# Graph layer and expert layer on one core: row numbers of the first chunk found on chip, down products ahead of the third tile's up products, turned halves kept apart

## The reference, cut

```python
def ln(x): ...                                   # over the 1024 columns
h   = ln(x) @ W.T + b                            # x 1250 x 1024
agg = segment_sum(norm[:, None] * h[col], row)   # 20000 edges and one loop per node
x   = x + agg
y   = ln(x)
logits = y @ router_w.T + router_b               # 8 experts
topk_vals, topk_idx = top_k(logits, 2); topk_w = softmax(topk_vals)
for e in range(8):                               # w1 512 x 1024, w2 1024 x 512
    cw  = sum(where(topk_idx == e, topk_w, 0), -1)
    out = out + (gelu(y @ w1[e].T + b1[e]) @ w2[e].T + b2[e]) * cw[:, None]
return x + ln_w_b(out + y)
```

## Time and profile before

| | us |
| --- | --- |
| median of the runs | 623.88 (621.68 to 625.24) |
| span of the profiled execution | 619.0 |
| PE busy in the span | 533.6 (86%) |
| DVE busy | 470.0 (76%) |
| ACT busy | 242.4 (39%) |
| POOL busy | 193.9 (31%) |
| aggregate loop | 183 to 283.9 |
| first chunk up to the second chunk's up products | 283.9 to 343.7 |

### The profile page before, as it was taken

The page is one execution under the profiler, slowest core; times in us unless marked ns, Lnnn a source line. Parts: engine busy times, 40 slices in busy tenths (PEclk is TensorE's granted clock), DMA queues, the critical chain, the costliest instruction groups (busy, mean ns, idle before and its releaser), DMA issues.

```text
span 619.0 us, 12317 instructions
## 1 busy us (share of the span) xinstructions
PE 533.6 (86%) x3660; PEld 298.1 (48%) x3661; DVE 470.0 (76%) x1295; ACT 242.4 (39%) x358; POOL 193.9 (31%) x199
## 2 busy tenths in 40 slices
PE   1688999899999999995779999999999999999100
PEld 1244554445444555554564655556565656564000
DVE  8879869997174889898858778695868685755397
ACT  5333444324280243435534344343444443401470
POOL 3013000000001165656544535344452543151240
PEclk9999999999899999998699999999999999999655
DMA  6894320333327243445486969798897889173978
GB/s 234 326 380 139 58 46 10 72 77 60 57 95 279 103 158 141 167 138 201 127 303 168 271 211 233 251 231 254 219 263 200 260 222 284 28 166 77 263 209 279
DMA packets 59565, 112.34 MB, mean 181 GB/s; under 512 B 33490, under 2 KB 33903, under 8 KB 59504
## 3 DMA queue, kind: packets, MB, share of 16 engines
q1 hardware_dynamic: 49424, 80.02, 37.7%
q0 software_dynamic: 8896, 27.38, 21.3%
q10 hardware_dynamic: 1184, 4.20, 2.0%
HBM read 71.75 MB, written 33.67 MB: 170 GB/s over the span
## 4 chain that ended last, share of the span: by engine, by line
PE 77%; DVE 14%; issue 3%; DMA 2%; ACT 2%; DVEq 1%; POOL 0%; ACTq 0%; POOLq 0%; SPq 0%
PE ps L1794 7%; PE ps L1795 7%; PE ps L1913 7%; PE ps L1914 6%; PE ps L1915 6%; PE ps L1892 5%; PE ps L1893 5%; PE ps L1894 5%; PE ps L1703 4%; PE ps L1642 4%; PE ps L1705 4%; PE ps L1704 4%; PE ps L1874 4%; DVE wbufs L1279 2%; PE ps L1623 2%
## 5 line engine op out<-in xcount | busy, mean ns | idle before, releaser
L613 POOL DMA_INDIRECT acc_rows<-work,ids_out x24 | 53.0, 2208 | 106.1 <-DVE work L1497 106.1
L1794 PE MATMUL ps<-wbufs,rows_and_counts 128*128 128x512 f16 x200 | 75.8, 379 | 0.5 <-DVE wbufs L1279 0.5
L1892 PE MATMUL ps<-rows_and_counts,wbufs 128*128 128x336 f16 (+2 forms) x256 | 74.9, 298 | 1.4 <-DVE rows_and_counts L1437 0.8
L1795 PE MATMUL ps<-wbufs,rows_and_counts 128*128 128x512 f16 x200 | 75.8, 379 | 0.0
L1893 PE MATMUL ps<-rows_and_counts,wbufs 128*128 128x336 f16 (+2 forms) x256 | 74.9, 298 | 1.0 <-issue 1.0
L1894 PE MATMUL ps<-rows_and_counts,wbufs 128*128 128x336 f16 (+2 forms) x256 | 74.9, 298 | 0.0
L1913 PE MATMUL ps<-wbufs,rows_and_counts 128*128 (+1 forms) x192 | 72.9, 379 | 1.6 <-issue 1.3
L1452 DVE SCALAR_TENSOR_TENSOR wbufs<-stage,wbufs 128x1024 f16<-128x1024 f32 x56 | 67.2, 1218 | 8.4 <-ACT wbufs L927 8.3
L1914 PE MATMUL ps<-wbufs,rows_and_counts 128*128 (+1 forms) x192 | 72.8, 379 | 0.0
L1915 PE MATMUL ps<-wbufs,rows_and_counts 128*128 (+1 forms) x192 | 72.8, 379 | 0.0
L526 POOL TENSOR_TENSOR work<-work 128x1024 f16<-128x1024 f32 x9 | 19.2, 2130 | 168.9 <-ACT work L900 168.9
(11 more groups left out here) (308 smaller groups left out, 1054.1 us busy)
## 6 DMA issues: line engine op xcount, KB each, us to landing
stage<-wst_in SPq DMA_DIRECT2D x72, 512.0 KB
acc_rows<-work SPq DMA_DIRECT2D x10, 512.0 KB
x_rows<-work SPq DMA_DIRECT2D x10, 512.0 KB
t<-x_in SPq DMA_DIRECT2D x1, 4096.0 KB, 14.0
wbufs<-b_in ACTq DMA_DIRECT2D x8, 512.0 KB
wbufs<-acc_rows SPq DMA_DIRECT2D x8, 512.0 KB, 6.2
t<-x_in SPq DMA_DIRECT2D x1, 3072.0 KB, 11.6
t<-x_in SPq DMA_DIRECT2D x1, 2048.0 KB, 7.8
```

Source lines behind the costliest of these rows:

```text
L1794: mm(o, ct_hi[:, cs], hs[:, at:at + HALF], start=(m == 0), stop=False, skip_group_check=True)
L1795: mm(o, ct_hi[:, cs], hs[:, D + at:D + at + HALF], start=False, stop=False, skip_group_check=True)
L1892: mm(o, wbufs[:, ds(w + ws, P)], x_hi, start=(j == 0), stop=False)
```

## The change

- Row numbers of the first chunk are found on chip. For each tile DVE sums the two masks of expert 0 (`chosen`) and compares the tile's slots with 0 to 383 (`slot_hot`, 128x384 in f16, only the third tile's columns from tile 7 on); PE multiplies that with a column of row numbers (`number`, three products one column wide); DVE adds the tiles up (`ids_known`). SP's two reads of the slot table for it go. POOL gathers the first two tiles in iteration 8 (before: 9, behind the aggregate's end), the third in iteration 11.
- DVE places tile 6 inside `add_agg(8)`, tile 7 between the halves of `add_agg(9)`, and chooses for tile 8 behind the normalized row of tile 9. PE ranks tile 7 inside `aggregate(9, 1)`.
- The weight pieces of expert 0 are split in iterations 0 to 7 (before: 2 to 9), on POOL directly behind `xs_lo` and ahead of the scatters.
- Turned halves stay apart: high and low are transposed into places of their own in PSUM, in f16. For a row tile ACT copies the high half and DVE the low one; for a chunk ACT copies both and DVE's subtractions (L1365, L1437) go.
- First chunk: PE multiplies the first two tiles up between the last turnings, goes down for tile 0 (parts 0 and 1), turns the third tile, part 2, third tile up, part 3, then turns the second chunk between parts 4 and 5. The gelus of the first two tiles come on their own. On DVE two pieces stand ahead of the halves of the first two tiles.

```diff
@@ POOL, the loop
             for r in range(NT + 2):
                 if r < NT - 1:
                     xs_lo(NT + r)
+                if r < PIECES:
+                    split_lo(PIECES + r, e_hi[0], e_lo[0])
                 if 2 <= r:
-                    if r - 2 == FIRST_TILES:
-                        pool.wait_ge(agg_done, 2 * NT)
+                    if r - 1 == FIRST_TILES:
                         pool.wait_ge(x2_first_stored, 16 * FIRST_TILES)
-                        pool.wait_ge(ids_in, 16)
+                        pool.wait_ge(first_ids_done, 1)
                         for i in FIRST:
-                            gather_first(i, ids_first, FIRST_TILES)
+                            gather_first(i, ids_known, FIRST_TILES)
+                    if r == NT + 1:
+                        ...
+                        pool.wait_ge(third_id_done, 1)
+                        ...
                     pool.wait_ge(slots_done, r - 1)
                     ...
-                if 2 <= r < NT:
-                    split_lo(PIECES + r - 2, e_hi[0], e_lo[0])
@@ ACT, the loop (the high half of the piece moves in the same way)
-            for r in range(NT + 1):
+            for r in range(NT):
                 ...
+                if r < PIECES:
+                    split_hi(PIECES + r, e_hi[0])
+            turn_copied(0)
+            turn_copied(1)
+            x2t_hi(NT - 1)
+            turn_copied(2)
+            turn_copied(3)
             act.wait_ge(gap_done, 1)
@@ DVE
             def x2t_lo(r):
-                dve.wait_ge(x2t_hi_done, r + 1)
-                v.tensor_tensor(x2t[:, D:], x2t_ps, x2t[:, 0:D], ALU.subtract).then_inc(x2t_lo_done, 1)
+                dve.wait_ge(x2t_done, r + 1)
+                dve.wait_ge(router_done, r)
+                v.tensor_copy(x2t[:, D:], x2t_ps[1]).then_inc(x2t_lo_done, 1)
@@
+                    if r == NT - 1 and n == 0:
+                        place(r - 2)
                 ...
+                if r == FIRST_TILES + 1:
+                    place(FIRST_TILES - 1)
                 ...
                 if r == NT - 1:
-                    x2t_lo(r - 1)
+                    choose(r - 1)
@@
-            def place(r):
+            def number_slots(r):
                 dve.wait_ge(rank_done, r + 1)
+                st3.did(v.tensor_tensor(chosen[:], choice(r)[:, 0:1], choice(r)[:, NE:NE + 1], ALU.add))
                 st3.link(v.tensor_tensor(slot_of[:], rank_ps[:, 0:NE], carry[:], ALU.add))
+                if r >= 2:
+                    dve.wait_ge(slot_hot_used, r - 1)
+                first = 0 if r < FIRST_TILES else FIRST_CH
+                v.tensor_scalar(slot_hot[r % 2][:, first:], slot_no16[:, first:], slot_of[:, 0:1], chosen[:],
+                                ALU.is_equal, ALU.mult).then_inc(slot_hot_done, 1)
+
+            def place_slots(r):
                 st3.link(v.tensor_tensor(slot_pick[:]...
@@
             for r in range(NT + 2):
-                if 2 <= r:
+                if r == FIRST_TILES + 2:
+                    dve.wait_ge(slot_hot_used, FIRST_TILES)
+                    st3.link(v.tensor_reduce(ids_sum[:, 0:len(FIRST)], ids_ps[:, 0:len(FIRST), 0:FIRST_TILES], AXX, ALU.add))
+                    v.tensor_copy(ids_known[:, 0:len(FIRST)], ids_sum[:, 0:len(FIRST)]).then_inc(first_ids_done, 1)
+                if 2 <= r and r != NT:
                     choose(r - 2)
@@
+            def first_chunk(split):
+                st4.enter(0)
+                for j in range(2):
+                    piece_lo(0, j, split)
+                for f in range(FK):
+                    dve.wait_ge(first_gelu_done, f + 1)
+                    halves_of(slice(f * CH, f * CH + FIRST_CH)).then_inc(y_lo_first, 1)
+                ...
+                for k in range(3):
+                    evict(0, k, 0)
+                    if 2 + k < EARLY:
+                        piece_lo(0, 2 + k, split)
+                for f in range(FK):
+                    dve.wait_ge(gelu_done, FK + f + 1)
+                    halves_of(slice(f * CH + FIRST_CH, (f + 1) * CH)).then_inc(y_lo_done, 1)
+                evict(0, 3, 0)
+                ...
@@ PE
+            def number(r):
+                pe.wait_ge(slot_hot_done, r + 1)
+                for i in range(CT) if r < FIRST_TILES else range(len(FIRST), CT):
+                    ins = mm(ids_ps[:, i, r:r + 1], slot_hot[r % 2][:, i * P:(i + 1) * P], token16[:, r:r + 1],
+                             start=True, stop=True)
+                ins.then_inc(slot_hot_used, 1)
@@
-            for r in range(NT + 2):
-                ...
+            for r in range(NT):
+                aggregate(r, 0)
+                if r >= 4:
+                    number(r - 4)
+                if r == FIRST_TILES + 2:
+                    number(FIRST_TILES - 1)
+                    pe.wait_ge(first_ids_done, 1)
                 if r >= 2:
                     route(r - 2)
+                if r == NT - 1:
+                    aggregate(r, 1, range(NT - 3))
+                    rank(r - 2)
+                    aggregate(r, 1, range(NT - 3, NT))
+                    turn2(r - 1)
+                    continue
+                aggregate(r, 1)
+                if r >= 1:
+                    turn2(r - 1)
                 if r >= 2:
                     rank(r - 2)
+            number(NT - 3)
+            route(NT - 2)
+            turn_first(0)
+            turn_first(1)
+            rank(NT - 2)
+            turn2(NT - 1)
+            up_first(0)
+            number(NT - 2)
+            route(NT - 1)
+            turn_first(2)
+            up_first(1)
+            rank(NT - 1)
+            up_first(2)
+            turn_first(3)
+            number(NT - 1)
+            for j in range(3, DK):
+                up_first(j)
@@
+            def first_chunk():
+                down_part(0, 0, 0)
+                down_part(0, 0, 1)
+                pe.wait_ge(third_in, 16)
+                turn_third()
+                down_part(0, 0, 2)
+                up_third()
+                down_part(0, 0, 3)
+                pe.wait_ge(chunks_done, 1)
+                pe.wait_ge(plans_done, 1)
+                following = entry_of(1)
+                turn4(1, 0)
+                turn4(1, 1)
+                for k in range(4, 2 * CT):
+                    down_part(0, 0, k)
+                    for j in range(3 * k - 10, 3 * k - 7):
+                        turn4(1, j)
+                return following
```

More of the change, by code:

```diff
@@ L936, in _ @@
             end_first = act.value_load(ranges2[0:1, 1, 0:1], min_val=1, max_val=MAXC - 2)
-            for j in range(DK):
-                turned(0, j, FIRST_CH)
+            for q in range(2):
+                third_copied(q)
             def chunk(c, e, split, first=False, last=False):
@@ L1379, in _ @@
                     v.engine_nop().then_inc(gap_done, 1)
-                if 2 <= r:
+                if 2 <= r and r - 2 not in (FIRST_TILES - 1, NT - 3, NT - 2):
                     place(r - 2)
@@ L1467, in _, with halves_of, evict @@
             v.tensor_copy(plans[:], plans_f[:]).then_inc(plans_done, 1)
-            for j in range(DK):
-                turned(0, j, FIRST_CH)
-            def chunk(c, e, h, split, first=False, last=False):
-                st4.enter(c * LINKS4)
-                if split is not None and not first:
+            def halves_of(fs):
+                st4.link(v.tensor_copy(y_hi[:, fs], y32[:, fs]))
+                return v.tensor_tensor(y_lo[:, fs], y32[:, fs], y_hi[:, fs], ALU.subtract)
+            def evict(c, k, h):
+                o = y_out[k // 2][:, k % 2 * HALF:(k % 2 + 1) * HALF]
+                dve.wait_ge(down_done, c * (2 * CT) + (k + 2))
+                v.scalar_tensor_tensor(o, down_ps[k % 2], 1.0 / WSCALE, b2_row[h][:, k % 2 * HALF:(k % 2 + 1) * HALF],
+                                       ALU.mult, ALU.add).then_inc(down_read, 1)
@@ L1475, in chunk @@
+            def chunk(c, e, h, split, last=False):
+                st4.enter(FK + c * LINKS4)
+                if split is not None:
                     for j in range(EARLY):
@@ L1782, in _, with aggregate @@
                 linear(NT - 1, quarter)
-            def aggregate(r, n):
+            def aggregate(r, n, ms=range(NT)):
                 o = agg_ps[r % 2][:, n * HALF:(n + 1) * HALF]
-                if r >= 2:
+                if r >= 2 and 0 in ms:
                     pe.wait_ge(var_done, len(NORM_GROUPS) + r - 1)
-                for m in range(NT):
+                for m in ms:
                     cs = slice(m * NP + r * P, m * NP + (r + 1) * P)
@@ new lines, in up_first, with turn_third @@
+            def up_first(j):
+                pe.wait_ge(first_turned, j // 2 + 1)
+                if j == 0:
+                    pe.wait_ge(w_lo_done, 2 * PIECES)
+                for f in range(FK):
+                    ins = first_products(j, f)
+                if j == DK - 1:
+                    ins.then_inc(first_up_done, 1)
```

(10 more changed lines are left out.)

375 lines of the change are left out of this document (205 added, 170 removed).

## The result

The changed kernel takes 642.14 us in the median (639.68 to 646.59), the kernel before 624.56 (621.68 to 626.11): 1.029 times as long, 95% interval 1.025 to 1.033. The forecast was slower, 633.2, with a range to 640.0: the sign held, the time came out 9 us above it. The profiled execution has a span of 640.2 against 619.0, 21.2 more; it took 641.91 in all, 1.7 more than its span, and so stands at its kernel's median.

What follows compares the result with a forecast made beforehand. TensorE was full until 283.9, leaving 283.9 to 325.7 to win. Loop +8.7, tiles 8 and 9 +2.55, tail −3.2, cold start +1.3 gave +9.35 on span 619.0; 4.88 more to the median made 633.2, range 622 to 640.

Steps and rivals of the forecast that it cites:

- Loop: Aggregate loop: held VectorE operations lengthen the period from 10.34 to 11.58 us, +8.7 over seven iterations.
- The hold: Aggregate loop: slots and cast on VectorE wait for the end of GpSimd's operations, to T+3.4 and T+5.6 from iteration start.
- The copy: Low half of the turned row, copied from PSUM instead of subtracted: 0.81 us taken against 1.22, saving 0.40 per iteration.
- The one-hot: Added VectorE operation over 384 columns for row numbers, ahead of the slots: 0.22 us taken, bounds 0.21 to 0.81.
- the term of 2.55: Tiles 8 and 9, with placing moved: 12.9 us against 10.35, +2.55, bounds 1 to 4.
- The tail: End of last normalized row to second chunk's up products: 52.1 us against 55.4, −3.2 before any cold start.
- half a cold start: TensorE possibly cold as the first tiles' up products start: costs 2.7 us, half taken, +1.3.
- A: Rival, aggregate loop: VectorE is not held, TensorE keeps the period at 10.34; 624.5 us, chance 0.20.
- C: Rival: VectorE not held and the hole ahead of the first down product closes; 617 us, chance 0.15.
- B: Rival: low-half copy stays at 1.22 us, 0.40 more in eight tiles, +3.2; 636.5 us, chance 0.20.

Runs made afterwards that it cites:

- a_pad40: Changed kernel with 40 unused semaphore increments on TensorE ahead of the first down product, where it waits anyway: 634.4 us, 7.7 less.
- b_split_ahead: Kernel before with only GpSimd's weight split moved directly behind the row's low half, ahead of the scatters: 634.25 against 622.82, ratio 1.019.

## Why the prediction was wrong in size

- **Loop: the mechanism right, its sum too high.** The hold was read from eight casts, and slots, cast and period came as worked out: 1.97 (to T+3.34) and 1.14 (to T+5.44), 11.29 against 11.58. The copy took 0.69, not 0.81. The Trainium skill, "VectorE: DVE Perf Modes", section "The perf-mode tier table", has a PSUM source at up to twice the base rate, from which the prediction estimated 0.66. The one-hot had its next start 0.29 later, not 0.22. The sum over seven iterations, +8.7, was too high: the end of the first normalized row to that of tile 7 is 71.46 before and 76.30 after, +4.8. Of the seven periods only the last five have both holds, and cost 0.9 to 1.0 each; that of tile 1, with no placing, gained 0.5, and that of tile 2 lost 0.7.
- **Tiles 8 and 9: the term of 2.55 was mis-sized.** They take 28.06 instead of 19.91, +8.15, where the sum had 2.55. By the rows, the holds cost 0.95 in tile 8 as in the tiles ahead of it, place(6) its 1.96, and the wait of PE for the row numbers 2.87, which was named in the term without a price of its own. The release of the turning of tile 8, 3.7 us late, was not in the sum at all (2.6 us of it went with two scatters out of the way). These four make 8.4, about what was measured. Loop and tiles together: 11.25 forecast, 13.0 measured, nearer than either part because one was too high and the other too low: that is luck.
- **The tail: the step that failed.** −1.9 was forecast (−3.2 and half a cold start), +5.9 measured. The largest part, 5.95 us, is a wait for code that no row of before shows at that place and that the sum had at nothing, without a bound: code that is rewritten was taken to cost no more than its instructions. With the code shifted (a_pad40) 1.17 us of it are left, and the tail is 57.5: still 2.2 longer than before, where a gain had been forecast. Most of the rest lies ahead of the first down product, which came 26.4 us behind T9 instead of 22.4: the end of the Exp (gap_exp) came at 15.3 instead of 12.0, because up_first ran on the cold clock (half rate, the lower of the two levels, from 300.0 to 310.2; the sum had half the price of this), DVE got the logits of route(9) 1.6 us behind its last product, and rank(9) waits for DVE's masks in the middle of the up products. The idle PE and the cold clock ahead of the first down product came as forecast (7.12 us, half rate from 327.3 to 334.1).
- **Rivals.** A and C needed a DVE that is not held; b_split_ahead shows masks held as well. B's condition, a copy as slow as the subtraction, did not come. The side was right for the reason given, in the loop; in the tail, where a gain was forecast, it was wrong. Two of the causes, late release and code, were in no rival.
- **The base.** The forecast set a change, worked out on one profile, on the median of before. Since that profile was a quick execution, the miss is 8.9 us in the time and 11.9 in the spans: −3.9 in the loop, +5.6 in tiles 8 and 9, +7.8 in the tail, and 2.4 of scatter ahead of the loop and behind.

## What to carry to other kernels

Before an operation is moved on GpSimd, look at what VectorE begins while it runs: here each held operation waited for GpSimd's end, however small it was, and two GpSimd operations without a break held two. Where a change rewrites the code of an engine with branches, a wait named "issue" behind a branch can be a cost of placement: shift the code, in a stretch where the engine waits anyway, before the change itself is judged. A stage that gets shorter is worth nothing until the waits that hand over to the next engine have been priced as well.

## Not expected of the hardware

- Held on DVE here, beside the cast: int32 from two operands (1.97), a mask of 8 columns (2.05), a sum of one column (1.99), a one-hot of 384 (2.15). Not held in the same stretches: reads from PSUM and the search for the maximum.
- PE's products were reported late while POOL issued indirect transfers in a row. Behind six in a row, ACT was released 2.4 to 4.1 us after the last product's end in seven of the profiles with that order, between 0.35 us ahead of the end of the sixth and 1.2 behind it; behind four in a row 1.1 to 1.2, and 0.03 where a gap split the six (tile 6 placed behind). That it goes with the transfers was shown by moving two scatters; what happens inside was not.
- 40 increments that nothing waits for changed the median by −7.7 us in one kernel and +3.9 in the other; the stretches behind them show −5.2 and +2.0 of this.
